# First cross-attention of a Perceiver kernel: 16 near-equal projection units per batch, and norm, queries and batch 0's projections in one block

## The reference

```python
h = layernorm(x)                                    # 16 x 64 x 256
q = heads(h @ wq + bq)                              # 16 heads of 16 dims
k, v = heads(ctx @ wk + bk), heads(ctx @ wv + bv)   # ctx: 16 x 1601 x 256
x = x + merge(softmax(q @ k.T / 4) @ v) @ wo + bo
```

## Time and profile before

| what | us |
|---|---|
| median of 3 runs (2579.84 to 2586.66) | 2581.17 |
| the profiled execution | 2583.49 |
| its span, first to last instruction | 2581.7 |
| TensorE busy | 2228.6 (86%) |
| VectorE busy | 1257.6 (49%) |
| ScalarE busy | 1001.7 (39%) |
| GpSimd busy | 309.4 (12%) |

### The profile page before, as it was taken

One profiled execution on the slowest core, in us unless ns is written; L12 is line 12 of the kernel. 1 busy time (PEld: TensorE's weight loads), 2 busy tenths in 40 slices (PEclk: granted clock), 3 DMA queues, 4 the chain that ended last, 5 costly groups with the idle time before them and its releaser, 6 DMA issues. The chain is left out here.

```text
span 2581.7 us, 39302 instructions
## 1 busy us (share of the span) xinstructions
PE 2228.6 (86%) x15444; PEld 1465.9 (57%) x15444; DVE 1257.6 (49%) x2219; ACT 1001.7 (39%) x1861; POOL 309.4 (12%) x353
## 2 busy tenths in 40 slices
PE   5899899999989976999998799967999997686695
PEld 2666666676666664555554577844555544445363
DVE  2455555555555543444444234436777743555013
ACT  0354444455544552333333011113666662332121
POOL 3222222222222200000000000031000001000202
PEclk9999999999999988999999889986999998796797
DMA  6766676666666631000000122123222203114212
GB/s 174 180 156 166 144 166 156 154 151 154 154 163 154 135 71 41 11 6 11 5 0 1 40 114 98 50 61 52 30 29 30 33 12 83 38 17 192 69 46 66
DMA packets 107749, 220.09 MB, mean 85 GB/s; under 512 B 58818, under 2 KB 75211, under 8 KB 101844
## 3 DMA queue, kind: packets, MB, share of 16 engines
q1 hardware_dynamic: 106036, 213.44, 34.7%
q0 software_dynamic: 1536, 4.20, 0.5%
HBM read 91.08 MB, written 19.27 MB: 43 GB/s over the span
## 5 line engine op out<-in xcount | busy, mean ns | idle before, releaser
L745 DVE TENSOR_REDUCE L_xattn_maxima<-L_xattn_scores 128x1 f32<-128x1024 f32 (+1 forms) x256 | 253.5, 990 | 270.4 <-PE L_xattn_scores L633 269.8
L813 ACT ACTIVATE L_xattn_probs_t<-L_xattn_turned 128x1024 f32<-128x1024 f32 (+1 forms) x256 | 220.7, 862 | 414.1 <-PE L_xattn_turned L645 414.1
L1604 DVE TENSOR_REDUCE shared_half_maxima<-shared_ring 128x1 f32<-128x1024 f32 (+1 forms) x256 | 248.7, 989 | 106.9 <-PE shared_ring L1518 103.6
L1677 ACT ACTIVATE shared_exps<-shared_scores 128x512 f32<-128x512 f32 (+1 forms) x416 | 225.6, 594 | 123.9 <-PE shared_scores L1539 123.3
L645 PE MATMUL L_xattn_turned<-ident,L_xattn_probs 128*128 128x128 f32 x1664 | 236.1, 282 | 28.2 <-ACT L_xattn_probs_t L813 27.4
L645 PEld LDWEIGHTS L_xattn_turned<-ident,L_xattn_probs 128*128 128x128 f32 x1664 | 196.9, 144 | 111.2 <-issue 91.4
L825 ACT ACTIVATE L_xattn_probs<-L_xattn_scores,L_xattn_maxima 128x1024 f32<-128x1024 f32 (+1 forms) x256 | 235.5, 925 | 37.2 <-DVE L_xattn_maxima L748 37.2
L603 PE MATMUL L_xattn_projected<-L_xattn_ctx,L_xattn_wk 128*128 128x512 f32 (+1 forms) x512 | 205.8, 524 | 17.4 <-DMA L_xattn_ctx<-in_ctx_t 10.9
L609 PE MATMUL L_xattn_projected<-L_xattn_wv,L_xattn_ctx 128*128 128x256 f32 (+1 forms) x832 | 202.0, 384 | 5.1 <-DVE L_xattn_v L720 4.7
L633 PE MATMUL L_xattn_scores<-L_xattn_k_stack,L_xattn_q_stack 128*128 128x512 f32 (+1 forms) x512 | 159.9, 394 | 36.1 <-ACT L_xattn_probs L825 29.5
L609 PEld LDWEIGHTS L_xattn_projected<-L_xattn_wv,L_xattn_ctx 128*128 128x128 f32 (+1 forms) x832 | 150.4, 186 | 33.2 <-DVE L_xattn_v L720 7.1
(11 more groups left out here) (351 smaller groups left out, 3027.1 us busy)
## 6 DMA issues: line engine op xcount, KB each, us to landing
L_xattn_k_stack<-L_xattn_k_part SPq DMA_DIRECT2D x512, 200.2 KB, 3.8
L_xattn_ctx<-in_ctx_t SPq DMA_DIRECT2D x16, 1602.0 KB, 6.9
ffn_task<-in_ffn_task SPq DMA_DIRECT2D x16, 1024.0 KB, 6.6
experts_w_in<-in_expert_in SPq DMA_DIRECT2D x8, 1024.0 KB, 11.4
shared_k<-k_scratch SPq DMA_DIRECT2D x64, 100.1 KB, 4.1
L_xattn_q_stack<-q_scratch SPq DMA_DIRECT2D x128, 32.0 KB, 2.1
k_scratch<-L_xattn_shared_part SPq DMA_DIRECT2D x128, 32.0 KB, 1.7
shared_q<-q_scratch SPq DMA_DIRECT2D x64, 64.0 KB, 4.3
```

Of the source, the lines that this page charges most:

```text
L745: nc.vector.reduce_max(maxima[n % 2][:, half:half + 1], cols, axis=AX).then_inc(halves_maxed, 1)
L813: nc.scalar.activation(probs_t[:, t:t + m, p * P:(p + 1) * P], turned_tiles[:, 0:m, :], ACT.Copy).then_inc(turned_moved, 1)
L1604: nc.vector.reduce_max(half_maxima[:, n, half:half + 1], ring_flat[:, HALF_STARTS[half]:HALF_STARTS[half + 1]], axis=AX).then_inc(ring_max ...
L1677: nc.scalar.activation(exps[n % 2][0:m, h * BANK:(h + 1) * BANK], scores[0:m, h, :], ACT.Exp, scale=SCALE).then_inc(exps_done, 1)
```

## The change

The keys of a group are cut into pieces of 400, 400, 400 and 402 columns. Keys units alternate with the others (shared, then the seven values units), so that each of the 16 slots of a batch has one unit; the turn of the shared values comes after the last pair's transposes. TensorE's wait for the last moved unit goes from the batch's first score to `weigh` of the first group. Norm, queries and the projections of batch 0 become one block, `first_block`, whose SyncE program also issues that batch's queries, key stacks and shared stores; there the units cycle through four banks. The helpers (`load_q`, `stack_keys`, `split_keys`, `move_projection` and others) move out of the engines' programs with the bank as an argument, unchanged but for the widths.

```diff
-    k_units = [(g, s) for g in range(GROUPS) for s in K_STARTS]
+    cuts = [EVEN_KEYS * i // (2 * CHUNKS_PER_GROUP) * 2 for i in range(CHUNKS_PER_GROUP + 1)]
+    k_units = [(g, s, e - s) for g in range(GROUPS) for s, e in zip(cuts, cuts[1:])]
-    units = ([("keys", i) for i in range(CHUNKS_PER_GROUP)] + [("shared", 0)]
-             + [("keys", i) for i in range(CHUNKS_PER_GROUP, K_UNITS)] + [("values", i) for i in range(V_UNITS)] + [("turn", 0)])
+    odd_units = [("shared", 0)] + [("values", i) for i in range(V_UNITS)]
+    units = [unit for i in range(K_UNITS) for unit in (("keys", i), odd_units[i])] + [("turn", 0)]
     U = len(units)
-    slots = [[i] for i in range(CHUNKS_PER_GROUP)] + [[i] for i in range(CHUNKS_PER_GROUP + 1, U)]
-    slots[CHUNKS_PER_GROUP - 1].append(CHUNKS_PER_GROUP)
...
+            with core.block() as block:     # first_block
+                def _(sp):
+                    for i in range(HALVES):
...
+                        sp.dma_start(x[:, half], dram["x"][:, half]).then_inc(x_loaded[i], 16)
+                    sp.dma_start(core.ident[:], dram["ident"]).then_inc(ident_loaded, 16)
+                    sp.dma_start(wk[:], dram[f"{layer}_wk"]).then_inc(keys_loaded, 16)
...
+                    load_ctx(sp, 0, 0)
+                    sp.dma_start(wq[:], dram[f"{layer}_wq"]).then_inc(query_loaded, 16)
...
+                    load_ctx(sp, 1, 1)
...
+                    for i, (m, half) in enumerate(q_units):
+                        for part, ready in ((0, high_ready), (1, low_ready)):
+                            sp.wait_ge(ready, i + 1)
+                            sp.dma_start(scratch[part, m, :, half * BANK:(half + 1) * BANK],
...
+                    sp.wait_ge(zeros_ready, 4)
+                    sp.wait_ge(query_stored, 16 * 2 * len(q_units))
+                    load_q(sp, 0, 0)
+                    load_q(sp, 1, 1)
+                    for n in range(PAIRS):
+                        if n % GROUP_PAIRS == 0:
+                            sp.wait_ge(keys_split, CHUNKS_PER_GROUP * (n // GROUP_PAIRS + 1))
+                        stack_keys(sp, n)
+                        if n == GROUP_PAIRS - 1:
+                            store_shared(sp, 0)
+                    sp.wait_ge(projection_done, U)
+                    load_ctx(sp, 2, 0)
+                    store_values(sp, 0, 0)
...
+                def _(pe):
+                    pe.wait_ge(ident_loaded, 16)
+                    for t in range(TILES):
+                        pe.wait_ge(rows_ready, t + 1)
+                        if t == TILES // 2:
+                            pe.wait_ge(x_turned_moved, 1)
...
+                    def project_first(u):
...
+                        project(pe, 0, 0, u, banks[:, u % 4], max(u - 3, 0) if units[u][0] != "turn" else u)
+                    for u in range(EARLY):      # EARLY = 3
+                        project_first(u)
+                    pe.wait_ge(query_loaded, 32)
+                    for i, (m, half) in enumerate(q_units):
+                        pe.wait_ge(x_turned_moved, half + 1)
+                        if i >= 2:
+                            pe.wait_ge(low_ready, i - 1)
...
+                        last.then_inc(query_done, 1)
+                        project_first(EARLY + i)
+                    for u in range(EARLY + len(q_units), U):
+                        project_first(u)
...
             def _(pool):
                 for i in range(2):
-                    nc.gpsimd.memset(q_stack[i][:].bitcast(F32), 0.0).then_inc(zeros_ready, 1)
...
-                for b in range(BATCH):
-                    batch(b)
-                    if b == 0:
+                for b in range(1, BATCH):
+                    split_parts(pool, b)
+                    if b == 1:
                         nc.gpsimd.tensor_tensor(core.x[:], core.x[:], bo[:].unsqueeze(1).to_broadcast([P, TILES, DIM]), ALU.add)
...
                 def weigh(b, parity, g):
+                    if g == 0:
+                        pe.wait_ge(projection_moved, U * (b + 1))
...
                         if n == 0:
                             pe.wait_ge(q_loaded[parity], 64 * (b - parity) + 128)
-                            pe.wait_ge(projection_moved, U * (b + 1))
                         score(b, parity, n, 0)
                         if not last:
-                            for u in slots[2 * n]:
-                                project(b + 1, 1 - parity, u)
+                            project(pe, b + 1, 1 - parity, 2 * n, projected[:, 0], U * (b + 1) + 2 * n)
...
+                        if n == PAIRS - 1 and not last:
+                            project(pe, b + 1, 1 - parity, U - 1, projected[:, 0], U * (b + 1) + U - 1)
-                for u in range(U):
-                    project(0, 0, u)
+                pe.wait_ge(bank_zeroed, 1)
                 pe.wait_ge(fold_ready, 1)
...
+                nc.vector.memset(projected[:, 0, :], 0.0).then_inc(bank_zeroed, 1)
```

More of the change, by code:

```diff
@@ new lines, in split_parts, with project @@
+        def split_parts(pool, b):
+            for what, i in units:
+                if what == "keys":
+                    split_keys(pool, b, i)
+                if what == "shared":
+                    split_shared(pool, b)
+        def project(pe, b, parity, u, bank, moved):
+            if u == 0:
+                pe.wait_ge(ctx_loaded[parity], 8 * (b - parity) + 16)
+            if moved > 0:
+                pe.wait_ge(projection_moved, moved)
+            what, n = units[u]
+            if what == "keys":
+                g, s, w = k_units[n]
+                for k in range(CHUNKS):
+                    last = nc.tensor.matmul(bank[:, 0:w], wk[:, k, g * P:(g + 1) * P],
+                                            ctx[parity][:, k, s:s + w], start=k == 0, stop=k == CHUNKS - 1)
+            if what == "values":
+                for i, t in enumerate(v_units[n]):
+                    rows = P if t < KEY_TILES - 1 else LAST_KEYS
+                    for k in range(CHUNKS):
+                        last = nc.tensor.matmul(
+                            bank[0:rows, i * DIM:(i + 1) * DIM],
+                            ctx[parity][:, k, t * P:t * P + rows], wv[:, k, :],
+                            start=k == 0, stop=k == CHUNKS - 1)
+            if what == "shared":
+                for k in range(CHUNKS):
+                    for c, s in enumerate(K_STARTS):
+                        w = min(BANK, EVEN_KEYS - s)
+                        last = nc.tensor.matmul(
+                            bank[PAIR_ROWS * c:PAIR_ROWS * (c + 1), 0:w], w_shared[:, k, :], ctx[parity][:, k, s:s + w],
+                            start=k == 0, stop=k == CHUNKS - 1, skip_group_check=True)
+            if what == "turn":
+                for j in range(BANK // P):
+                    last = nc.tensor.transpose(bank[:, j * P:(j + 1) * P], shared_full[:, j * P:(j + 1) * P], core.ident[:])
+            last.then_inc(projection_done, 1)
@@ L425, in cross_attention_block @@
+        with ExitStack() as first:
+            first_block(first)
         probs = [sb(f"probs{i}", [P, KEYS_PADDED]) for i in range(2)]
@@ L480, in _ @@
             def _(sp):
[L481 to L507, removed]
                 def batch(b, parity, ctx_left, q_left):
@@ L780, in batch @@
                         if not last:
-                            for u in slots[2 * n]:
-                                move_projection(b + 1, 1 - parity, u)
+                            move_projection(dve, b + 1, 1 - parity, 2 * n, projected[:, 0])
                         maximum(b, n, 1)
@@ L788, in batch @@
                         if not last:
-                            for u in slots[2 * n + 1]:
-                                move_projection(b + 1, 1 - parity, u)
+                            move_projection(dve, b + 1, 1 - parity, 2 * n + 1, projected[:, 0])
+                        if n == PAIRS - 1 and not last:
+                            move_projection(dve, b + 1, 1 - parity, U - 1, projected[:, 0])
                         if n == GROUP_PAIRS:
```

370 lines of the change are left out of this document (224 added, 146 removed).

## The result

| | before | changed |
|---|---|---|
| median, us | 2583.91 (2579.84 to 2589.17, 4 runs) | 2505.3 (2503.12 to 2509.65, 4 runs) |
| ratio | | 0.9697, 95% interval 0.9676 to 0.9718 |
| profiled execution, span, us | 2583.49, 2581.7 | 2509.65, 2507.8 |

What follows compares the result with a forecast made beforehand. Batches 1 to 14 decide: first halves bound by TensorE's unit, second by the score-maximum-exponential chain. Start +4.8, batch 0 -2.4, loop -78.9 sum to -76.5: 2505 us, range 2494 to 2526.

Steps and rivals of the forecast that it cites:

- First halves: In a pair, first score matmul to second: TensorE busy throughout, paying for its unit; 3.06 us to fall to 2.685.
- second halves: In a pair, second score matmul to the next pair's first: forecast to stay at 2.94 us with a full unit.
- the chain: Beside TensorE in second halves: scores, VectorE's maximum, ScalarE's exponential, which the next score waits for; 2.94 us.
- the double slot: Pair 1's second half before, holding 66-column keys and shared units: 5.23 us instead of 2.94; ending it forecast at 32 us.
- The start: Everything up to batch 0's first score, now one block: first score near 84.5 instead of 79.66, +4.8 us.
- SyncE's serial piece: In the first block, SyncE's issues of queries, stacks, shared keys, context and values: 45.5 us from 37.5.
- the lower bound: Of the start's cost: +2 us if the queries issue faster with no load beside them.
- Rival 3: First block slower: TensorE at 1.2 GHz up to q3, SyncE's piece starting 14 us later; 2519 us, chance 0.13.
- Batch 0: First batch, starting with TensorE idle and at 1.2 GHz: 50.0 us instead of 52.44, -2.4.
- it costs nothing at either place: Wait for the last projection result, moved from the batch's first score to its first weighing: claimed free at both.
- Rival 4: Slower than before: SyncE's queue becomes the batch, growing from 40 to 57.3 us; 2624 at 60 a batch, chance 0.03.
- The same 16 shared matmuls take 3.46: Pair 1 before: in ten of fourteen batches they take 3.46 instead of 1.92 us at a granted clock of 0.58.

Runs made afterwards that it cites:

- e1: The changed kernel with the keys cut as before, 512, 512, 512 and 66 columns a group: 2526.1 us, ratio 0.9776.
- e2: The changed kernel with the old key cuts and the old order of units, still one unit a slot: 2543.4 us, ratio 0.9845.
- a0_changed: The changed kernel run again, unedited, as reference for the follow-up runs: 2506.6 us, ratio 0.9701 of the kernel before.
- e3: The changed kernel with TensorE's wait for the last moved projection result put back ahead of each batch's first score: 2511.1 us, ratio 0.972.
- e8: The changed kernel with each batch's shared stores issued five times, 19.2 us more of SyncE's issues a batch: 2604.4 us, ratio 1.0078.
- e6: The changed kernel with its first block's SyncE program ending behind batch 0's queries and the first group's stacks, the rest issued next block: 2477.8 us, ratio 0.9592.

## Why the prediction was right

**The loop: right in mechanism and size.** First halves pay by columns (2.68 for 2.685; e1's 3.05 and 2.14), second halves are held by the chain at 2.94, the double slot cost its idle stretch and the clock behind it (e2). -73.9 for the forecast's -78.9; the regular batch is 51.44, which would give -79.7, and the missing 5.7 us are longer halves in batches 1 and 5 (the stops, and in batch 1 a low clock: 5.2 us) and in batches 6 and 13. By the traces of batches 1 to 14 the three parts of the loop's change are 44.0 us for ending the double slot (before to e2; 48 forecast, with the clock), 13.8 for alternating (e2 to e1) and 17.8 for equal cuts (e1 to a0_changed); the last two were forecast at 30 together. Stops of some us blur all three. What the clock alone gave back is read from the batches of the kernel before (57.5 against 55.9); no run removes it without the double slot.

**The start: right that it costs, too large.** Forecast +4.8, measured +2.4. The queries were stored at 36.9 (37.5 forecast), and SyncE's serial piece took 43.6 us for 45.5: the queries' loads 7.4 instead of 9.5, which was the lower bound's reason. Rival 3 (TensorE at 1.2 GHz up to the last query product) did not come. Windows of the changed kernel, the four-bank stretch and the idle one behind it:

```profile
18.10:49.00 30.90, 30.28 (x117) 18.85 (x116) 13.29 (x21) 2.75 (x4) 13.99 (x18) 1.00 0.38 109
49.00:82.09 33.09, 0.00 (x0) 0.03 (x1) 1.08 (x4) 0.00 (x0) 0.74 (x6) 0.55 0.91 195
```

TensorE keeps its full clock (1.00) while it cycles through four banks, busy for 30.3 of the 30.9 us, and loses it when it stands idle. The Trainium skill ("TensorE: Matmul & The Clock Gate", A second HAM failure mode) reports a swinging clock for another kernel, in bf16, that cycles through PSUM banks; the trace here does not show it.

**Batch 0: forecast -2.4, measured -1.7**, with pair 0 at 8.2 instead of 7.4 us (6.84 before). Its first half runs at the low clock as forecast, but that costs more than the 0.56 us put down for the pair: 3.06 us against 1.85 before, at a granted clock of 0.50. Its keys unit, which takes 1.51 us in the loop:

```profile
83.08 2.87 PE L500 MATMUL L_xattn_projected<-L_xattn_ctx,L_xattn_wk 128*128 128x400 f32 x4
```

**What was luck.** The forecast fall of the span was 76.5, the measured one 73.9. The start came out 2.4 us better than forecast, batch 0 0.7 worse, the loop 5.0 worse and the rest 0.7 better, so that half of the errors cancel. That the median is 2505.3 for 2505 is luck besides: the four runs spread over 6.5 us, and the median before is 2583.91 here where the forecast went out from 2581.17.

**Wrong in detail:** "it costs nothing at either place" (the wait for the last projection result). With the turn last, the wait at the score would cost 0.25 us a batch (e3); at the weighing it costs nothing. Rival 4's bound of 57.3 us a batch should be about 56.9 (51.5 + 76.2/14). "The same 16 shared matmuls take 3.46" is batch 5's row; the ten batches with a low clock differ in it, and in five of them the low clock reaches into the next half, though each loses about the same 1.6 us. **Wrong in place:** rival 4's rule, that the queue becomes the batch, was right (e8), but its wait is VectorE's for the stacks' reads, not a score's for their writes. **Missed:** the stops. The trace of the kernel before has one, the 0.81 us above; that batch takes 58.5 instead of 57.5 us.

The profile had all that the sum needed, because outside pair 1 and such stops the halves repeat to 0.02 us. Where the forecast could have gone further is the first block: TensorE's 33 us of idle time was written down as +4.8 us of cost, but as a chance it is worth 29 (e6).

## What to carry to other kernels

Find for each short stretch of a loop which limit holds it, and put the long pieces of filler work where the engine that does them is the limit, in equal sizes; a piece under the floor of a stretch is wasted there, and two in one slot wait for each other. Before work is merged into one block, add up each queue's issues in it: the block lasts as long as the longest queue, and issues that nobody in it needs belong behind it. An idle stretch of two microseconds can cost nearly as much again in clock.

## What the runs showed of the hardware

TensorE's clock fell after one idle stretch of 1.88 us in ten of fourteen batches, for about 1.6 us each; in the batches of e1 and e2, which lack that stretch and have the same matmuls, it did not fall. An idle stretch of that length is not always enough: the other four batches kept a clock of 1.00, and a stop of 1.94 us in batch 1 lowered the clock in a0_changed but not in e3.

TensorE also stopped for 0.3 to 2 us with nothing to wait for in the profile, mostly inside the 104 small matmuls of a weighing, and mostly while the key stacks kept the DMA engines busy (a share of 1.04 in the window above, 0.75 inside the stop of 1.93 us). With a third of the stacks' bytes one stop of 0.5 us was left, with more transfers they grew (11.3 us in the weighings of e8), but there is one of 0.81 us at a share of 0.03, and e6 has none in its loop at 0.75. What stops TensorE no run shows.
